# Score maxima into the queries' row by DMA, maxima moved within a pair, token transposes as plain matmuls

## The reference

```
x   = x + proj_w . softmax(theta(x) . phi(x) / sqrt(64)) . x          # non-local block, no biases
t   = tokens(x);  z = layernorm(t)
t   = t + softmax(Q(z) . K(z) / sqrt(128)) . V(z)                     # self attention, with biases
z   = layernorm(t)
t   = t + sum over the 2 best of 8 experts of w_e * (gelu(z W1e + b1e) W2e + b2e)
out = tokens back to channels
```

## Time and profile before

| what | value |
|---|---|
| runs shown, median | 570.67 us (570.37, 570.67, 576.16) |
| the profiled execution's own time | 572.82 us |
| its span, first to last instruction | 570.9 us |
| granted TensorE clock, mean of the span | 0.878 |
| busy: PE, DVE, ACT, POOL | 74%, 68%, 52%, 57% |
| step -1 (pairs) | 21.3 to 42.2 us |
| step 0 | 42.2 to 75.3 us |
| step 3, with the W1 rows | 148.4 to 188.5 us |
| step 5 | 222.9 to 256.2 us |
| end of step 7's GpSimd work to the end of the scatters | 324.5 to 402.5 us |

### The profile page before, as it was taken

The page is one execution under the profiler, slowest core; times in us unless marked ns, Lnnn a source line. Parts: engine busy times, 40 slices in busy tenths (PEclk is TensorE's granted clock), DMA queues, the critical chain, the costliest instruction groups (busy, mean ns, idle before and its releaser), DMA issues.

```text
span 570.9 us, 14104 instructions
## 1 busy us (share of the span) xinstructions
PE 421.9 (74%) x3966; PEld 299.9 (53%) x3967; DVE 387.9 (68%) x1106; ACT 297.6 (52%) x599; POOL 323.0 (57%) x358
## 2 busy tenths in 40 slices
PE   5566778889499999999979448100398988999436
PEld 3333355565365565666646346000287977989312
DVE  3675746866766777777675877730188979889547
ACT  5536767767378866767737311500154545555102
POOL 8001215546344668645539977777147878788810
PEclk9878879999989999999989759655699999999955
DMA  5820031000000000600000011141313223322166
GB/s 184 191 32 2 0 105 44 1 3 0 0 1 0 2 2 1 184 2 1 0 2 15 14 58 53 52 112 62 81 35 92 82 80 87 83 83 82 47 223 233
DMA packets 35025, 33.22 MB, mean 58 GB/s; under 512 B 8486, under 2 KB 27945, under 8 KB 34985
## 3 DMA queue, kind: packets, MB, share of 16 engines
q1 hardware_dynamic: 30378, 23.22, 14.6%
q0 software_dynamic: 4608, 9.51, 5.0%
HBM read 18.98 MB, written 13.73 MB: 57 GB/s over the span
## 4 chain that ended last, share of the span: by engine, by line
PE 39%; POOL 23%; issue 14%; DVE 10%; ACT 9%; DMA 3%; ACTq 0%; POOLq 0%; SPq 0%; DVEq 0%
PE PV L574 13%; POOL zbuf L478 11%; PE SC L574 10%; PE MX L574 9%; POOL ybuf L562 6%; PE PR L574 4%; ACT E L990 3%; DVE mxb L1279 3%; ACT EH L991 3%; POOL EL L519 2%; ACT QK L907 2%; DVE TOK L1533 1%; PE PR L621 1%; DVE TOK L1538 1%; POOL carry L560 1%
## 5 line engine op out<-in xcount | busy, mean ns | idle before, releaser
L519 POOL TENSOR_TENSOR EL<-E,EH 128x1024 f32 (+1 forms) x32 | 69.0, 2156 | 66.3 <-ACT EH L991 66.3
L574 PE MATMUL PV<-VH,EH 128*128 128x129 f16 x512 | 103.3, 230 | 2.0 <-POOL EL L519 1.2
L574 PE MATMUL PV<-VH,EL 128*128 128x129 f16 x512 | 102.0, 225 | 0.0
L574 PE MATMUL PV<-VL,EH 128*128 128x128 f16 x512 | 101.9, 224 | 0.0
L574 PE MATMUL SC<-QK 128*128 128x512 f16 x320 | 92.8, 394 | 10.8 <-ACT QK L907 9.4
L562 POOL DMA_INDIRECT ybuf<-QK,yid x80 | 86.6, 1082 | 18.3 <-issue 12.5
L990 ACT ACTIVATE E<-SC 128x512 f32<-128x512 f32 x128 | 77.5, 606 | 32.5 <-PE SC L574 20.1
L1279 DVE TENSOR_REDUCE mxb<-MX 128x1 bf16<-128x1024 f32 x64 | 78.1, 1221 | 9.7 <-PE MX L574 9.4
L991 ACT ACTIVATE EH<-SC 128x512 f32 (+1 forms) x128 | 78.4, 613 | 0.0
L478 POOL DMA_INDIRECT zbuf<-ZZ,posi x64 | 66.3, 1036 | 18.9 <-issue 18.9
L574 PE MATMUL MX<-EL,EH 128*128 x640 | 59.4, 246 | 1.6 <-DVE QK L1490 1.6
(11 more groups left out here) (200 smaller groups left out, 886.4 us busy)
## 6 DMA issues: line engine op xcount, KB each, us to landing
EH<-zbuf SPq DMA_DIRECT2D x40, 130.0 KB, 2.2
X<-in_x_dram SPq DMA_DIRECT2D x4, 512.0 KB, 5.4
zbuf<-zer SPq DMA_DIRECT2D x16, 128.0 KB, 3.3
X<-in_L_ffn_W_dram SPq DMA_DIRECT2D x1, 2048.0 KB
EL<-ybuf SPq DMA_DIRECT2D x4, 512.0 KB, 5.6
EH<-ybuf SPq DMA_DIRECT2D x4, 512.0 KB, 10.1
out_dram<-X SPq DMA_DIRECT2D x8, 256.0 KB, 3.5
ybuf<-QK,yid POOLq DMA_INDIRECT x80, 2.3
```

What stands on the lines that cost most here:

```text
L519: nc.gpsimd.tensor_tensor(EL[:, u % 2, ds(i * 2, 2), c], E32h[1], EH[:, u % 2, ds(i * 2, 2), c], ALU.subtract).then_inc(e32_free[1], 1)
L574: return nc.tensor.matmul(o, w, r, start=start, stop=stop)
```

## The change

Four edits, and some moves of weight work:

1. `row` is gone on TensorE and ScalarE, and so are negI and its preparation on GpSimd. VectorE's maxima go to mx (fp32, one column for each 128 queries). After pairs 1 and 3 of a step, `scaled(h)` multiplies four columns by minus one over the constant into mx16 (fp16), and SP issues four DMAs (`row`), each of 128 elements of 2 bytes from 128 partitions into one row of 128 queries of QL. TensorE waits on row_in[0] before the first scores of a step and on row_in[1] before the scores of the second half of the queries.
2. The maxima of a pair are moved: on TensorE the first from behind the second half's scores to ahead of `outputs(i, 0)`, the second from the pair's end to behind `values`; on VectorE accordingly.
3. The fp16 token transposes become matmuls with the identity as the moving operand, with fp32 output in PSUM.
4. The first pair's order of `residual_stream`, `high_x` and, in step 7, of `rank` and `transposes`; ScalarE's order of `values` and the third exponential; VectorE's order in the pair.
5. `expert_rows` goes into the pairs of step 3, one in each; ScalarE's `first_weights` moves to step 4, GpSimd's `low_weights` to step 5; SP issues the W1 load after the first row of m = 2.

```diff
+            def row(m, h):
+                sp.wait_ge(mx_scaled, 2 * m + h + 1)
+                for t in range(PAIRS):
+                    c = h * HALF + t * P
+                    sp.dma_start(QL[0:1, m % 3, c:c + P], mx16[:, h, t:t + 1]).then_inc(row_in[h], 16)
+            for m in range(UNITS):
+                row(m, 0)
+                if m == 2: (waits, then the load of W1)
+                row(m, 1)
+                if m == 2: (wait for W1, then the load of b1)
...
@@ TensorE
-                            last = nc.tensor.transpose(o_[:, at:at + P], ZZ[:, ds(t, 1), h * P:(h + 1) * P], ident16[:])
+                            last = mm(o_[:, at:at + P], ZZ[:, ds(t, 1), h * P:(h + 1) * P], ident16[:], True, True)
                 def pair(i, first):
+                    if first and u is not None:
+                        pe.wait_ge(row_in[0], 16 * PAIRS * (u + 1))
                     if u is not None:
                         scores(i, 0, 0)
+                    if first and v is not None and v < B:
+                        residual_stream()
                     if v is not None and v >= B and not (first and late_rank):
                         transposes(i)
                     if u is not None:
                         scores(i, 1, 0)
-                    if first and u is not None:
-                        row(u, mx_base(s) + 1)
-                    if not first and m is not None:
-                        row(m, i * 3 + n_mx)
-                    if first and v is not None and v < B:
-                        residual_stream()
+                    if m is not None:
+                        maxima(i, 0)
                     if a is not None:
                         outputs(i, 0)
-                    if u is not None:
-                        if first:
-                            pe.wait_ge(mx_free, mx_base(s) + 2)
-                        scores(i, 0, 1)
                     if first and late_rank:
                         rank(0)
                         transposes(i)
-                    if m is not None:
-                        maxima(i, 0)
+                    if first and u is not None:
+                        pe.wait_ge(row_in[1], 16 * PAIRS * (u + 1))
+                    if u is not None:
+                        scores(i, 0, 1)
                     if v is not None and v < UNITS:
                         values(i)
+                    if m is not None:
+                        maxima(i, 1)
                     if u is not None:
                         scores(i, 1, 1)
...
@@ ScalarE
                     if u is not None:
                         exponentials(i, 0, 0)
                     if first and v is not None and v < B:
+                        residual_stream()
                         high_x()
...
+                    if u is not None:
+                        exponentials(i, 0, 1)
                     if v is not None and v < UNITS:
                         values(i)
                     if u is not None:
-                        exponentials(i, 0, 1)
                         exponentials(i, 1, 1)
...
@@ VectorE, the new order of a pair
+    maxima(i, 0); newton_square, newton_slope; e_low(i); newton_end; sums(i, 0); values(i); residual(i, 0);
+    maxima(i, 1); written(i, 0), statistics(i, 0); scaled(i // 2) if i is odd; queries(i); counted, moments(i, 0);
+    sums(i, 1); keys(i); logits(i); residual(i, 1); expert_rows(i) if s == 3; written, statistics, moments(i, 1)
```

More of the change, by code:

```diff
@@ L207, in build @@
         mx_free = sem("mx_free")
+        mx_scaled = sem("mx_scaled")
+        row_in = [sem(f"row_in{h}") for h in range(2)]
         sc_full = sem("sc_full")
@@ L584, in _ @@
                 n_mx = mx_pairs(s)
-                def row(unit, need):
-                    pe.wait_ge(mx_free, need)
-                    for p in range(2):
-                        last = mm(MX[0:1, p * P:(p + 1) * P], mxb[:, p:p + 1], negI[:, layer(unit), :], True, True)
-                    last.then_inc(mx_full, 1)
                 def residual_stream():
@@ L747, in pair @@
                         scores(i, 1, 0)
-                    if first and u is not None:
-                        row(u, mx_base(s) + 1)
-                    if not first and m is not None:
-                        row(m, i * 3 + n_mx)
-                    if first and v is not None and v < B:
-                        residual_stream()
+                    if first and m is not None:
+                        for h in range(3):
+                            pe.wait_ge(pr_free[h], uses_before(m + 1, h) + 1)
+                    if m is not None:
+                        maxima(i, 0)
                     if first and a is not None:
@@ L767, in pair @@
                         transposes(i)
-                    if first and m is not None:
-                        for h in range(3):
-                            pe.wait_ge(pr_free[h], uses_before(m + 1, h) + 1)
-                    if m is not None:
-                        maxima(i, 0)
+                    if first and u is not None:
+                        pe.wait_ge(row_in[1], 16 * PAIRS * (u + 1))
+                    if u is not None:
+                        scores(i, 0, 1)
                     if first and v is not None and v < B:
@@ L1002, in pair @@
                 def pair(i, before, first=False):
+                    late = first and s == UNITS - 1
                     if u is not None:
@@ L1005, in pair @@
                     if first and v is not None and v < B:
+                        residual_stream()
                         high_x()
-                    late = first and s == UNITS - 1
+                    if first and s == -1:
+                        later_weights()
                     if v is not None and v >= B and not late:
@@ L1242, in _ @@
                     dve.wait_ge(mx_free, mx_pairs(a - 2) + 1)
-                if s == 3:
-                    dve.wait_ge(w1_in, 16 * (2 + E))
-                    for k in range(PAIRS):
-                        expert_rows(k)
                 def low(o, i_, hi, scale=1 / WS):
@@ L1370, in pair @@
                 def pair(i, before):
-                    if on_a:
-                        sums(i, 0)
+                    if on_m:
+                        maxima(i, 0)
+                    if before is not None:
+                        newton_square(*before)
+                        newton_slope(*before)
                     if on_u:
@@ L1375, in pair @@
                     if before is not None:
[L1376 to L1377 removed]
+                        newton_end(*before)
                     if on_a:
[L1379 to L1385 removed]
+                        sums(i, 0)
                     if on_v and v < UNITS:
@@ L1388, in pair @@
                     if on_a:
+                        residual(i, 0)
+                    if on_m:
+                        maxima(i, 1)
+                    if on_a:
+                        written(i, 0)
                         statistics(i, 0)
-                        sums(i, 1)
-                        counted(i, 0)
+                    if on_m and i % 2 == 1:
+                        scaled(i // 2)
                     if on_v and v < UNITS:
@@ L1407, in pair @@
                     if on_a:
+                        residual(i, 1)
+                    if s == 3:
+                        dve.wait_ge(w1_in, 16 * (2 + E))
+                        expert_rows(i)
+                    if on_a:
+                        written(i, 1)
+                        statistics(i, 1)
                         counted(i, 1)
```

81 lines of the change are left out of this document (30 added, 51 removed).

## The result

Over 20 runs each the changed kernel took 575.78 us (573.29 to 582.62) and the kernel before 573.06 us (568.14 to 655.19): a ratio of 1.0059, 95% interval 1.0037 to 1.0082. A kernel has a few slower executions (one of 655.19 us here), and all ratios leave them out. The forecast was 558.5 us, the range 545 to 572. The change costs some 0.6% where it was to bring two per cent.

What follows compares the result with a forecast made beforehand. No engine full overall: a chain of waits bounds steps -1 and 0, TensorE step 5, a W1 stall lengthens step 3. Terms sum to -12.2 us: profiled 572.8 to 560.6, 558.5 against the median; range 545 to 572.

Steps and rivals of the forecast that it cites:

- The row by DMA: Heads of steps 2 to 6: the row's second half arrives 4.6 us after scaling, TensorE waits some 0.7 each, +3.5 us.
- Cover: Heads of steps -1, 0, 1 and 7: the wait for x, or the router in step 7, hides the row's wait.
- rival 3: All eight heads: the row's second half arrives late, each us over 4.6 paid eight times, up to 599 us; chance 0.10.
- rival 2: Steps 2 to 6: VectorE's order sets the pace at 8.8 us a pair, +10 us, giving 568.5; chance 0.18.
- Starts: Start of steps -2 and -1: ScalarE copies TOK before rounding x, +3.0 and +1.1 us.
- Steps -1 and 0: Without the row in MX, pairs shorten to 4.25 us in step -1 (-3.8) and 5.4 in step 0 (-5.1).
- Step 1: Its head loses the row's matmuls and copy, about 1.2 us, three other pairs some 0.3 each: -2.1 us.
- Steps 2 to 6, twenty pairs: Two fewer TensorE matmuls a pair against VectorE's later low queries: pairs of 8.3 us, no gain, 0.
- Steps 3 and 4: Step 3 without the W1 stall, its work spread over pairs, -3.3 us; step 4 takes over ScalarE's weight copies, +1.0.
- Step 7's head: The last reduction leaves the way to `choose`, and `rank` no longer stands behind scores waiting for the row copy: -3.0 us.
- Transposes as plain matmuls: Token transposes: identity matmuls cost as the transposes did, with the same 128 columns and an equally wide copy: 0.
- The scaling and what stands ahead: VectorE's scaling before the row's DMA and the work ahead of it take 0.3 us of the row's 4.6.

Runs made afterwards that it cites:

- a1: Changed kernel without the row's DMAs and TensorE's waits for them, maxima not subtracted; last attention mark 302.87 us, fastest execution 609.92 against 614.36 for the kernel before.
- d1: c1 with the scaling as a scalar_tensor_tensor instruction; ratio to the kernel before 1.0183, last attention mark 326.24 us.
- d2: d1 with ScalarE rounding x before it copies TOK, as in the kernel before; fastest execution 606.20 us against 612.43, last attention mark 317.27.
- e1: Changed kernel with c1's transfer and each maximum scaled from PSUM right behind its reduction; 548.33 us against 574.71 for the kernel before, ratio 0.9528.
- e2: e1 with ScalarE rounding x before it copies TOK, as in the kernel before; 541.57 us against 574.71 for the kernel before, ratio 0.9432.
- d4: Kernel before, old order, with the row sent by one 4-byte-piece DMA a pair and d1's scaling; fastest execution 594.23 us against 612.43.
- a2: Kernel before with only the W1 rows worked on a pair at a time and the weight work moved; fastest execution 605.62 us against 614.36.
- a3: Changed kernel with the fp16 token transposes as transposes again; first five marks within 0.2 us of the changed kernel's, last attention mark 332.66, 4.5 later.
- c1: Changed kernel with the row sent by one DMA of 4-byte pieces a pair, scaled once a pair by a product; fastest execution 612.29 us against 614.59.

## Why the prediction was wrong

**The step that failed** is "The row by DMA". Its mechanism was named (the second half is needed some 4 us into the next step), its size and its cover were not.

- Size. I took "4 us plus 0.3 of hand-over and 0.3" for the scaling: 4.6. It was 7.8 at step 5's head: 0.45 from the scaling's start to the first issue, 1.80 for three issues and 5.6 for the last landing. Issues and landing together, 7.4, lie inside the bounds that I had written, 3.9 to 9.1; I took a value at their very bottom because the queue was idle. (Even that was misread: the earlier trace rows has a DMA share of 0.27 in step 5.) The landing alone had been bounded by 2.0 and 4.3 us, from 64 KB and from 8-byte pieces; 2-byte pieces into one partition lie beyond both, 4.5 in the median. The nearest rows were not near in the one property that counts, and what spoke against 2-byte pieces was written down and given no weight because 8-byte pieces did not show it. The time of need was right: at step 5's head TensorE was ready for the row 4.1 us after the scaling's start, so 4.6 would have left 0.5 us of wait, and 7.8 left 3.7. (The 0.7 in the sum doesn't follow from its own terms: 1 + 4.6 - 4.2 is 1.4, or 1.1 if the scaling isn't counted twice.)
- Cover. "In steps -1, 0 and 1 the wait for x covers it, in step 7 the router." It did not: the heads of steps 0, 1 and 7 wait 4.36, 4.37 and 1.52 us. The wait came to 28.0 us instead of 3.5. It is rival 3, given 0.10, with the sign that it named, a wait of several us ahead of the second half's scores, and its "from 1.5 us over the whole gain is gone" was passed at 3.2 us over. Its formula gives 3.2 x 8 - 12.2 = +13 us, and the kernel lost about 3: by a1 the other terms brought 21.6 us at the mark instead of 15.7, and the wait cost 25.3 where the formula has 25.6 + 3.5. That the time came out close to the kernel before, which the forecast had given 0.18 as rival 2, is the chance sum of a large loss and a large gain; VectorE's order as rival 2 has it, +0.5 us in each pair, is not seen.

**The other terms.**

- Starts: +4.1 forecast, +4.0 at the first maxima in the changed kernel (25.34 against 21.31), 4.7 by d1 and d2, 4.0 by e1 and e2. Right, and it stays to the end (7.3 us at the last mark from e1 to e2).
- Steps -1 and 0, -3.8 and -5.1: right in kind. Three pairs of step 0 in e1 take 5.23 to 6.41 us and in e2 5.24 to 5.38, where I had 5.4. In the changed kernel one of them was 6.71, with a held scaling of 1.73 us in it. From the first maxima to the mark of step 0 the forecast was -8.9; it is -4.3 in the changed kernel, whose head of step 0 waits 4.36 for the row, -6.4 in e1 and -8.3 in e2.
- Step 1, -2.1: too small. It is -7.7 in e1 (31.39 against 39.07), -2.9 in the changed kernel with its wait. I priced the row there at its own instructions; what I missed is the ring through MX, in which every later maximum waited. The same holds for the old row as a whole, whose replacement brings 21 us in d4.
- "Steps 2 to 6, twenty pairs: 0", against -4.4 and +10. The three looped pairs of steps 5 and 6 are unchanged in the changed kernel (25.05 and 22.54 us against 25.12 and 22.64); in e1 they are 24.80 and 21.48. My value was right for the kernel as it was made. That e1 is 0.3 and 1.1 us faster there suggests that held scalings, which I had not seen, took part of what TensorE had to give; no run shows it by itself. (The 0.22 us for two matmuls was a single one's duration; the two are busy for 0.27.)
- Steps 3 and 4, -3.3 and +1.0: a2, which has this part alone, gives -8.5 and +2.5, and +1.2 in step 5 that I had at 0; with +1.3 scattered over the other steps its last mark is 3.5 earlier. The stall was worth more and its work came back more. The forecast's -3.3 is 6.5 for the stall and 0.8 for half clock behind it, less 3.0 and 1.0; no run shows the 0.8. In a2 the granted clock of step 3 goes from 0.92 to 1.00 as its length goes from 41.4 to 32.9 us, stall and clock together. In the new order the W1 rows are held too (8.95 us for four).
- Step 7's head, -3.0: -1.7 in the changed kernel, of which the row's wait takes 1.52; -4.4 in e1.
- Transposes as plain matmuls, 0: right by a3.
- "The scaling and what stands ahead", 0.3 us: a mis-sized term that was costed by its 128x4 elements and not by what runs beside it. It also delays the row itself: two of the long ones are the scaling of a second half. In the changed kernel it adds 10.3 - 16 x 0.17 = 7.6 us to VectorE's time, mostly where VectorE had slack or TensorE waited for the row anyway; in c1, with 37.2 us in all, it took back nearly all that the faster row had won.

## What to carry to other kernels

A small transfer is priced by its piece and its target: look for a row with the same bytes a piece and the same partitions, and if there is none, let the bound reach beyond the nearest rows and time one alone first. When a value is needed early in the next stage, add issue, hand-over and landing from the moment it is ready to the first reader, and count on no cover that you can't point at. An instruction on a few numbers can cost what its neighbour engine's longest instruction costs: see which operands it reads from SBUF while GpSimd works, and move them to PSUM or move the instruction.

## What the hardware showed that was not expected

- A DMA of 128 pieces into one partition landed in 4.5 us with pieces of 2 bytes, in 2.0 with pieces of 4, and in 1.8 with 2-byte pieces into 128 partitions; 256 numbers as 4-byte pieces into one row took 1.9 us. Issues on SP, four in a row, were 0.60 us apart.
- VectorE instructions on 2 or 4 numbers a partition that read SBUF twice, or once as fp32 tensor_scalar, were held to within 0.03 us of the end of a GpSimd tensor_tensor: up to 2.0 us for 0.16. With the input in PSUM none of 64 was held. VectorE's W1 rows of 128x1024, with two SBUF inputs, ended 1.1 us behind such an instruction instead of running beside it. The profile shows the hold as busy time of the instruction, not as idle time before it.
